# A state space mixer's step pipeline: the masked products of two token tiles side by side, y and z made one step later

## The chip, the cores and the metric

The kernel runs on one core of a Trainium2 chip, as one launch. The metric is the device time of that launch in microseconds, median of three runs. The engines' names are those of the profile: PE (matrix products; PEld its weight loads), DVE (vector), ACT (scalar), POOL (GpSimd), SP (issues the DMAs).

## The reference

Input x is 1024 tokens by 512. Four blocks follow one another, each on the layer norm of x and added to it: a linear attention read-out, a mixture of LoRA experts, a state space mixer, a second LoRA block. Nearly all of the time, and the whole change, is in the third:

```python
proj = hidden_states @ in_proj_w.T
gate, hBC, dt = proj[..., :INTER], proj[..., INTER:INTER + CONV_DIM], proj[..., INTER + CONV_DIM:]
hBC = silu(causal_conv_4_taps(hBC))          # x (8192), B and C (8 groups of 128 each)
dt = softplus(dt + dt_bias);  A_dt = -exp(A_log) * dt;  x_dt = x * dt
Y_diag = einsum('bclsh,bcshp->bclhp', (C B^T) * L, x_dt)      # masked product inside a chunk of 128
Y_off  = einsum('bclhn,bchpn->bclhp', C, states_of_earlier_chunk) * exp(A_cumsum)   # across product
y = Y_diag + Y_off + D * x
y = rmsnorm(y) * norm_w * silu(gate)
return y @ out_proj_w.T
```

## The kernel before

**Groups and steps.** The mixer has 128 heads of 64 columns in 8 groups. One group is 18 column tiles of 128 of the input projection (B, C, 8 of x, 8 of the gate) and two halves of 8 heads. The kernel runs a hand-written pipeline over the groups: a lead of 8 steps (`kind` "lead"), then 16 steps `s` for each group `g` ("first", six times "middle", "last"). A step is one token tile `t = s % 8` of one half of the heads, together with a share of the projection of tiles that the following steps and the next group need. All five engines run the same loop of steps, each with its own list of what it does in a step, and they meet only through counted semaphores. Within an engine all is done in the order written.

**PE in step s.** `turn(s + 1)`: four transposes of x into PSUM bank 6 (L1827). `diag(s)`: the masked product of this token tile, 8 heads with 64 weight columns each, in two column halves of the array, into bank 4 (L1837; the trace has 16 rows, since each of these fp32 products is two). In odd steps `across(s)`: the product with the state of the earlier chunk, four products of 128 columns into bank 5 (L1854). Then one projection tile, `project`: 24 products of 512 columns into a bank pair of 0 to 3 (L203 to L205). Last `add_up(s - 1)`: the output product of the token tile before, 8 products with z_h (L1865, L1866) and four with z_l (L1869), into bank 7. Steps 10 and 12 have a second projection tile behind it (`PROJECTED`, tiles 11 and 14). Steps 14 and 15 also hold `within` (L1916) and the across part of C B^T (L1963) for the next group.

**DVE in step s.** `add_out(s - 2)` adds bank 7 to the sum (L1569). `times_dt(s + 1)` (L1580), in steps 1 and 9 the low part of the output weights, `wo_low` (L1587), then the three taps of the convolution of a projected tile, `taps` (L1558). Then y of this token tile: in odd steps the across product is scaled (L1641), D x and the masked product are added (4 of L1653), in odd steps also the across part (L1663), and z = y times gate (L1669). Then `mask(s + 2)` (L1602). In steps 10 and 12 the taps of a second tile follow (the table `LATE`: tiles 10 and 13).

**ACT in step s.** Eviction of the projected tile (`evict`, L1300 or L1308) and the high part of the weights of tile m + 2 (`w_high`, L1288); in steps 1 and 9 `wo_high` (L1333); `decay(s + 2)` (L1321, L1326); silu of the convolved tile after DVE's taps (L1312); for `LATE` tiles eviction and w_high once more; the square of y (L1394) and z_h, the high part of z (L1397).

**POOL in step s.** The low part of the weights for each tile of `EARLY[s] + LATE[s]` (`w_low`, L1215, which waits for ACT's w_high), then z_l (L1236, which waits for z_h), three additions of squares, and in odd steps the chunk-end weights (L1225).

```python
PROJECTED = [[n] for n in range(10)] + [[10, 11], [12], [13, 14], [15], [16], [17]]
EARLY = [[-1]] + [[n] for n in range(10)] + [[11], [12], [14], [15], [16]]
LATE = [[]] * 10 + [[10], [], [13], [], [], []]
```

Of the kernel before, what the change touches and what calls it, by code (L numbers as in the profile page):

```python
# [45 lines left out]
def f(ap):  # L46

    return ap.bitcast(F32)
# [730 lines left out]
def ssm_block(nc, ctx, sems, n, x_saved, ident, bank, acc, xh, xl, xdt, w_bufs, w_in, w_dt, par, dt_bias, a_log, w_out,  # L779
# [9 lines left out]

    def sb(name, shape, dt=F32):  # L790
        return ctx.enter_context(nc.sbuf_tensor("m_" + name, shape, dt))
# [234 lines left out]

    def has_tile(kind, m):

        return kind != "last" if m >= LEAD else kind != "lead"
# [37 lines left out]
    with nc.Block() as block:  # L1067
        @block.sync
        def _(sp):
# [88 lines left out]
            def step(g, s, kind):  # L1158
# [9 lines left out]
                if own(kind) and ahead(kind, s + ROW_BUFS):  # L1168
                    sp.wait_ge(diag_done, at(g, s))
                    load_rows(g, s + ROW_BUFS)  # L1170
# [5 lines left out]
                if s % 2 == 1 and own(kind) and ahead(kind, s + 4):  # L1176
                    sp.wait_ge(y_ready, at(g, s))
                    load_e(g, s + 4)
# [12 lines left out]
        def _(pool):  # L1191
# [36 lines left out]

            def step(g, s, kind):
                t = s % NT  # L1230
# [3 lines left out]
                if own(kind):  # L1234
                    pool.wait_ge(zh_ready, at(g, s))
                    nc.gpsimd.tensor_tensor(z_l[:, s % 2, :, :], zg[:], f(z_h[:, s % 2, :, :]),  # L1236
                                            ALU.subtract).then_inc(zl_ready, 1)
                    pool.wait_ge(sq_ready, at(g, s))
                    nc.gpsimd.tensor_tensor(ysq[:, 0:2, :], ysq[:, 0:2, :], ysq[:, 2:4, :],
                                            ALU.add).then_inc(sq_pair, 1)  # L1240
                    pool.wait_ge(sq_pair, g * STEPS + (s + 1))
                    nc.gpsimd.tensor_tensor(sq_acc[:, t, :], sq_acc[:, t, :], ysq[:, 0, :],
                                            ALU.add).then_inc(sq_first, 1)
                    pool.wait_ge(sq_first, g * STEPS + (s + 1))
                    nc.gpsimd.tensor_tensor(sq_acc[:, t, :], sq_acc[:, t, :], ysq[:, 1, :],
                                            ALU.add).then_inc(sq_summed, 1)
# [37 lines left out]
        def _(act):  # L1284
# [77 lines left out]

            def step(g, s, kind):
# [27 lines left out]
                if own(kind):  # L1391
                    act.wait_ge(y_ready, at(g, s))
                    act.wait_ge(sq_summed, at(g, s - 1))
                    nc.scalar.activation(ysq[:], y[:], ACT.Square).then_inc(sq_ready, 1)  # L1394
                    act.wait_ge(z_ready, at(g, s))
                    act.wait_ge(out_done, at(g, s - 2))
                    nc.scalar.activation(z_h[:, s % 2, :, :], zg[:], ACT.Copy).then_inc(zh_ready, 1)  # L1397
# [66 lines left out]
        def _(dve):  # L1464
# [126 lines left out]
            def cb_evict(part):  # L1591
                nc.vector.tensor_tensor(cb[:, part * CT:(part + 1) * CT, :],
                                        bank[:, 5, :].rearrange("p (b c) -> p b c", c=P),
                                        causal[:].unsqueeze(1).to_broadcast([P, CT, P]),
                                        ALU.mult).then_inc(cb_ready, 1)
# [8 lines left out]

            def step(g, s, kind):
# [7 lines left out]
                if s == 0 and own(kind):  # L1613
                    nc.vector.tensor_copy(par_dn[:], par_all[:, bass.ds(g, 1), CONV_PAR:PAR].rearrange(
                        "p a b -> p (a b)")).then_inc(dn_par_ready, 1)
                    dve.wait_ge(dn_par_ready, g + 1)
# [5 lines left out]
                if s == STEPS - 1 and kind != "last":  # L1622
                    dve.wait_ge(cb_last_done, g + 2)
                    cb_evict(1)
                if ahead(kind, s + 1) and s != STEPS - 1:
                    times_dt(g, s + 1)
                if own(kind) and t == 1:
# [8 lines left out]
                if own(kind):  # L1636
                    if s % 2 == 1:
                        dve.wait_ge(off_done, pair(g, s))
                        dve.wait_ge(e_loaded[s // 2 % 2], (g * 4 + (s // 4 + 1)) * 32)
                        off = e[:, s // 2 % 2, :, :]  # L1640
                        nc.vector.tensor_tensor(off, bank[:, 5, :].rearrange("p (c l) -> p c l", c=CT), off,  # L1641
                                                ALU.mult).then_inc(off_ready, 1)
                    dve.wait_ge(diag_done, at(g, s))
                    dve.wait_ge(ecs_stored, 16)
                    dve.wait_ge(sq_ready, at(g, s - 1))
                    dve.wait_ge(z_ready, at(g, s - 1))
                    whole = bank[:, 4, :].rearrange("p (c l) -> p c l", c=CT)
                    by_tensor = kind == "last" and half == 1
                    if by_tensor and s % 2 == 0:
                        last = nc.vector.tensor_copy(y[:], whole)  # L1650
                    for ct in range(0 if by_tensor else CT):
                        d = half * CT + ct
                        last = nc.vector.scalar_tensor_tensor(  # L1653
                            out=y[:, ct, :], in0=xc[:, half, ct, t * P:(t + 1) * P], scalar=par_dn[:, d:d + 1],
                            in1=bank[:, 4, ct * P:(ct + 1) * P], op0=ALU.mult, op1=ALU.add)
                    if by_tensor and s % 2 == 1:
                        dve.wait_ge(off_ready, pair(g, s))
                        last = nc.vector.tensor_tensor(y[:], whole, off, ALU.add)
                    elif s % 2 == 1:
                        last.then_inc(dx_added, 1)  # L1660
                        dve.wait_ge(dx_added, g * (STEPS // 2) + (s // 2 + 1))
                        dve.wait_ge(off_ready, pair(g, s))
                        last = nc.vector.tensor_tensor(y[:], y[:], off, ALU.add)  # L1663
                    last.then_inc(y_ready, 1)
                    dve.wait_ge(y_ready, at(g, s))
                    dve.wait_ge(zl_ready, at(g, s - 1))
                    if t == 0:
                        dve.wait_ge(gate_done, gate_at(g, half * LEAD - 1))
                    nc.vector.tensor_tensor(zg[:], y[:], gate[:, half, :, t * P:(t + 1) * P],  # L1669
                                            ALU.mult).then_inc(z_ready, 1)  # L1670
# [135 lines left out]
        def _(pe):  # L1806
# [24 lines left out]
            def diag(g, s):  # L1831
                pe.wait_ge(mt_ready, at(g, s))
                pe.wait_ge(xdt_ready, at(g, s))
                pe.wait_ge(y_ready, at(g, s - 1))
                for h in range(UH):
                    row = (h % 2) * SP_
                    last = nc.tensor.matmul(bank[row:row + SP_, 4, (h // 2) * P:(h // 2 + 1) * P],  # L1837
# [279 lines left out]
```

## Time and profile before

| | |
|---|---|
| median of 3 runs | 1736.9 us (1736.45 to 1739.39) |
| the profiled execution, its own time | 1737.69 us |
| its span, first to last instruction | 1735.9 us |
| mean granted TensorE clock | 0.987 |
| busy: PE, PEld, DVE, ACT, POOL | 1684.0, 1378.6, 1190.5, 1269.4, 732.2 us |
| PE's share of the chain that ended last | 81% |

A row of a timeline gives the start in us from the span's beginning, the length, the engine, the line in the kernel, what is written and read, and how many instructions were merged; in brackets the idle time of the engine before it and who ended it. "L1837 128*64" is a product that uses half of the array's columns. Rows of the clock view give the granted share of TensorE's clock in a stretch: 1.00 is 2.4 GHz, 0.50 is 1.2 GHz.

### The profile page before, as it was taken

What the parts mean: (1) busy time and instruction counts of PE and PEld (TensorE: products, weight loads), DVE (VectorE), ACT (ScalarE), POOL (GpSimd) and SP (SyncE); (2) the same over time, 40 slices, a digit from 0 to 9 for tenths busy, and PEclk for the clock granted to TensorE, in tenths of its full rate; (3) what the DMA queues carried; (4) which work ended last, traced back from release to release, by engine and by line L of the source; (5) the groups of instructions that cost most, each with busy time, mean ns of one, the idle gap of its engine ahead of it and who ended that gap; (6) DMA issues with size and microseconds to landing.
All of it is one profiled execution on the core that took longest, in us unless ns stands there. A gap on an engine that the chain in (4) does not pass through costs nothing.

```text
span 1735.9 us, 26827 instructions
## 1 busy us (share of the span) xinstructions
PE 1684.0 (97%) x9484; PEld 1378.6 (79%) x9484; DVE 1190.5 (69%) x1846; ACT 1269.4 (73%) x2171; POOL 732.2 (42%) x792
## 2 busy tenths in 40 slices
PE   6998799999999999999999999999999999999999
PEld 5876577888888888888888888888888888888877
DVE  5665676767676767667776767676767676767785
ACT  4333148987888779877987798778887889688851
POOL 3553122544344334443444444434443444344470
PEclk9998799999999999999999999999999999999999
DMA  4320225423232323332333232323232233223311
GB/s 170 109 68 1 75 65 159 122 93 105 86 112 85 117 74 111 95 109 83 113 93 107 78 110 88 116 88 109 94 110 78 86 115 104 90 79 115 105 70 49
DMA packets 98564, 166.46 MB, mean 96 GB/s; under 512 B 11616, under 2 KB 49888, under 8 KB 96768
## 3 DMA queue, kind: packets, MB, share of 16 engines
q1 hardware_dynamic: 98432, 164.75, 29.7%
q8 instruction: 76, 1.25, 0.3%
q14 instruction: 56, 0.46, 0.1%
HBM read 158.43 MB, written 6.29 MB: 95 GB/s over the span
## 4 chain that ended last, share of the span: by engine, by line
PE 81%; DVE 4%; ACT 2%; issue 1%; DVEq 0%; ACTq 0%
PE bank L203 15%; PE bank L205 15%; PE bank L204 15%; PE bank L1837 7%; PE bank L1865 7%; PE bank L1866 7%; PE bank L1869 7%; PE bank L1854 4%; PE bank L1827 3%; PE bank L1916 1%; DVE m_xc L1558 1%; DVE m_gate L1558 0%; PE bank L1845 0%; ACT m_mt L1321 0%; DVE m_xc L1492 0%
## 5 line engine op out<-in xcount | busy, mean ns | idle before, releaser
L203 PE MATMUL bank<-xh,w_h 128*128 128x512 f32 x1152 | 463.3, 402 | 3.4 <-DVE m_xc L1558 2.9
L205 PE MATMUL bank<-xh,w_l 128*128 128x512 f32 x1152 | 451.8, 392 | 0.0
L204 PE MATMUL bank<-xl,w_h 128*128 128x512 f32 x1152 | 449.4, 390 | 0.0
L1236 POOL TENSOR_TENSOR m_z_l<-m_zg,m_z_h 128x512 fp32r<-128x512 f32 x128 | 177.6, 1387 | 568.6 <-ACT m_z_h L1397 568.6
L1321 ACT ACTIVATE m_mt<-m_mt,m_unit 128x128 f32<-128x128 f32 x1024 | 312.1, 390 | 0.0
L1215 POOL TENSOR_TENSOR w_l<-w_raw,w_h 128x512 fp32r<-128x512 f32 x144 | 187.7, 1303 | 230.9 <-ACT w_h L1288 230.9
L1569 DVE TENSOR_TENSOR x<-x,bank 128x512 f32<-128x512 f32 x128 | 87.8, 686 | 264.5 <-PE bank L1869 264.5
L203 PEld LDWEIGHTS bank<-xh,w_h 128*128 128x128 f32 x1152 | 216.8, 188 | 55.7 <-issue 13.6
L205 PEld LDWEIGHTS bank<-xh,w_l 128*128 128x128 f32 x1152 | 216.5, 188 | 47.3
L1558 DVE SCALAR_TENSOR_TENSOR m_xc<-bank,m_par_conv,m_xc 128x1020 f32<-128x1020 f32 (+2 forms) x192 | 244.6, 1274 | 10.4 <-ACT m_xc L1300 5.4
L204 PEld LDWEIGHTS bank<-xl,w_h 128*128 128x128 f32 x1152 | 217.1, 188 | 41.7
L1865 PE MATMUL bank<-m_wo_h,m_z_h 128*128 128x512 f32 x512 | 203.8, 398 | 1.3 <-DVE x L1569 1.3
L1866 PE MATMUL bank<-m_wo_l,m_z_h 128*128 128x512 f32 x512 | 202.5, 396 | 0.0
L1602 DVE TENSOR_TENSOR m_mt<-m_mt,m_cb 128x1024 f32<-128x1024 f32 x128 | 156.9, 1225 | 26.1 <-ACT m_mt L1326 26.0
L1837 PE MATMUL bank<-m_mt,xdt 128*64 128x128 f32 x2048 | 140.1, 279 | 0.1
L1869 PE MATMUL bank<-m_wo_h,m_z_l 128*128 128x512 f32 x512 | 138.5, 392 | 0.0
L1326 ACT ACTIVATE m_mt<-m_mt 128x1024 f32<-128x1024 f32 x128 | 135.8, 1061 | 2.2
L1653 DVE SCALAR_TENSOR_TENSOR m_y<-m_xc,m_par_dn,bank 128x128 f32<-128x128 f32 x480 | 133.9, 342 | 1.5 <-PE bank L1837 1.5
L1837 PEld LDWEIGHTS bank<-m_mt,xdt 128*64 128x64 f32 x2048 | 109.2, 136 | 21.5 <-issue 20.5
L1580 DVE TENSOR_TENSOR xdt<-bank,m_unit 128x512 f32<-128x512 f32 x128 | 87.8, 686 | 49.5 <-issue 48.6
L1326 ACT ACT_TABLE_LOAD x93 | 119.3, 1283 | 1.6
L1865 PEld LDWEIGHTS bank<-m_wo_h,m_z_h 128*128 128x128 f32 x512 | 96.1, 188 | 24.2 <-ACT m_z_h L1397 1.3
(275 smaller groups left out, 2781.0 us busy)
## 6 DMA issues: line engine op xcount, KB each, us to landing
m_mt<-ncs_rows SPq DMA_DIRECT2D x128, 512.0 KB, 3.7
w_raw<-w_in SPq DMA_DIRECT2D x144, 256.0 KB, 3.0
m_wo_raw<-w_out_in SPq DMA_DIRECT2D x64, 256.0 KB, 5.1
m_e<-ecs_rows SPq DMA_DIRECT2D x128, 128.0 KB, 3.5
a_wo_raw<-wo_in SPq DMA_DIRECT2D x8, 1024.0 KB, 4.9
x<-x_in SPq DMA_DIRECT2D x8, 256.0 KB, 4.6
a_wq_raw<-wq_in SPq DMA_DIRECT2D x8, 256.0 KB, 4.1
x_saved<-x SPq DMA_DIRECT2D x1, 2048.0 KB, 9.1
```

Source lines behind the costliest of these rows:

```text
L203: nc.tensor.matmul(out, ah, bh, start=first, stop=False)
L204: nc.tensor.matmul(out, ah, bl, start=False, stop=False)
L205: return nc.tensor.matmul(out, al, bh, start=False, stop=last)
L1215: nc.gpsimd.tensor_tensor(w_l[:, m % 2, :, :], w_raw[:, m % W_BUFS, :, :], f(w_h[:, m % 2, :, :]), ALU.subtract).then_inc(w_split, 1)
L1236: nc.gpsimd.tensor_tensor(z_l[:, s % 2, :, :], zg[:], f(z_h[:, s % 2, :, :]), ALU.subtract).then_inc(zl_ready, 1)
L1321: last = nc.scalar.activation(mt[:, s % ROW_BUFS, h, :], mt[:, s % ROW_BUFS, h, :], ACT.Relu, bias=own_row)
L1326: nc.scalar.activation(slot, slot, ACT.Exp, scale=-1.0).then_inc(decay_ready, 1)
L1558: ins = nc.vector.scalar_tensor_tensor(out=dst[:, :, back:], in0=src[:, :, 0:length - back], scalar=par_conv[:, w:w + 1], in1=dst[:, :, ba ...
L1837: last = nc.tensor.matmul(bank[row:row + SP_, 4, (h // 2) * P:(h // 2 + 1) * P], xdt[:, s % 2, h * SP_:(h + 1) * SP_], mt[:, s % ROW_BUFS, ...
L1865: nc.tensor.matmul(bank[:, 7, :], z_h[:, s % 2, ct, :], wo_h[:, ct, :], start=ct == 0, stop=False)
L1866: nc.tensor.matmul(bank[:, 7, :], z_h[:, s % 2, ct, :], wo_l[:, ct, :], start=False, stop=False)
L1869: last = nc.tensor.matmul(bank[:, 7, :], z_l[:, s % 2, ct, :], wo_h[:, ct, :], start=False, stop=ct == CT - 1)
```

## The change

It holds for every group but the second half of the last one (`paired` is true). The arithmetic is the same.

1. PE: no masked product in an even step; the odd step does those of s - 1 and s, in banks 4 and 5 (`masked_in`).
2. The across product goes to bank 7, the output product's; it waits until bank 7 was added (`acc_added`), and the next output product waits until the across product was scaled (`off_ready`).
3. y and z of tile s - 1 are made in step s on DVE, ahead of times_dt and the taps; square and z_h on ACT in step s behind the decay and ahead of silu; z_l and the squares' sums on POOL in step s, behind `w_low` of `EARLY[s] + LATE[s]` (`made_in`). `add_up(s - 1)` stays in step s.
4. `within`, both parts, and the across part of C B^T stand in the middle of the projection of step 14.
5. In the last group's second half the old order stands; its step 8 makes y and z of tiles 7 and 8.

```diff
+    def paired(kind, s):
+        return not (kind == "last" and s >= NT)
+    def masked_in(kind, s):
...
+        if paired(kind, s):
+            return [s - 1, s] if s % 2 == 1 else []
+        return [s]
+    def made_in(kind, s):
...
+        if paired(kind, s):
+            return [s - 1] if behind(kind, s - 1) else []
+        return [s - 1, s] if s == NT else [s]
+    def across_bank(kind, s):
+        return 7 if paired(kind, s) else 5
...
@@ POOL
             def step(g, s, kind):
-                t = s % NT
                 for m in EARLY[s] + LATE[s]:
                     if has_tile(kind, m) and has_tile(kind, m + 2):
                         w_low(g, m + 2)
-                if own(kind):
-                    pool.wait_ge(zh_ready, at(g, s))
...
+                for made in made_in(kind, s):
+                    split_and_square(g, made)
@@ ACT
+                if paired(kind, s):
+                    for made in made_in(kind, s):
+                        square_and_high(g, made)
                 for m in EARLY[s]:
                     if has_tile(kind, m) and is_conv[m % TILES]:
                         silu(g, m)
...
                     if has_tile(kind, m):
                         evict(g, m)
                         w_high(g, m + 2)
-                if own(kind):
-                    act.wait_ge(y_ready, at(g, s))
...
+                if not paired(kind, s):
+                    for made in made_in(kind, s):
+                        square_and_high(g, made)
@@ DVE
-                if s == STEPS - 1 and kind != "last":
-                    dve.wait_ge(cb_last_done, g + 2)
-                    cb_evict(1)
+                if paired(kind, s):
+                    for made in made_in(kind, s):
+                        make_y(g, made)
+                        make_z(g, made)
+                    if own(kind) and s % 2 == 1:
+                        scale_across(g, s, kind)
                 if ahead(kind, s + 1) and s != STEPS - 1:
                     times_dt(g, s + 1)
...
@@ PE
             def diag(g, s):
...
-                pe.wait_ge(y_ready, at(g, s - 1))
+                by_tensor = g == LAST and s >= NT
+                to_bank = 4 if by_tensor else 4 + s % 2
+                if s == STEPS - 2 and not by_tensor:
+                    pe.wait_ge(cb_ready, g * 2 + 4)
+                pe.wait_ge(y_ready, at(g, s - 1 if by_tensor and s > NT else s - 2))
...
+            def across(g, s, kind):
...
+                if paired(kind, s):
+                    pe.wait_ge(acc_added, at(g, s - 2))
...
             def add_up(g, s):
...
+                if s % 2 == 0 and not (g == LAST and s >= NT):
+                    pe.wait_ge(off_ready, pair(g, s + 1))
...
             def step(g, s, kind):
...
-                if own(kind):
-                    diag(g, s)
...
+                for ready in masked_in(kind, s):
+                    diag(g, ready)
+                if own(kind) and s % 2 == 1:
+                    across(g, s, kind)
```

PE, a middle group: how an odd step begins. L1827 and L1888 are the transposes, L1837 and L1902 the masked products, L1854 and L1922 the across products. Before:

```order
L205 MATMUL bank<-xh,w_l 128x512
L1827 MATMUL bank<-ident,m_xc 128x128 x4
L1837 MATMUL bank<-m_mt,xdt 64x128 x8
L1854 MATMUL bank<-m_cb_across,m_xdd 128x128 x4
L203 MATMUL bank<-xh,w_h 128x512
```

Now:

```order
L204 MATMUL bank<-xl,w_h 128x512
L205 MATMUL bank<-xh,w_l 128x512
L1888 MATMUL bank<-ident,m_xc 128x128 x4
L1902 MATMUL bank<-m_mt,xdt 64x128 x16
L1922 MATMUL bank<-m_cb_across,m_xdd 128x128 x4
```

The masked products of two token tiles stand in a row; the even step has none (there the transposes are followed by the projection).

ACT, step 10 from its decay to the eviction of the next step (m_mt the decay, m_ysq the square of y, m_z_h the high part of z, the evictions read bank, silu reads and writes m_gate). Before:

```order
L1321 ACTIVATE m_mt<-m_mt,m_unit 128x128 x8
L1326 ACTIVATE m_mt<-m_mt 128x1024
L1312 ACT_TABLE_LOAD
L1312 ACTIVATE m_gate<-m_gate 128x1024
L1300 ACTIVATE m_gate<-bank,m_par_conv 128x1024
L1288 ACTIVATE w_h<-w_raw 128x512
L1394 ACTIVATE m_ysq<-m_y 128x512
L1397 ACTIVATE m_z_h<-m_zg 128x512
L1312 ACTIVATE m_gate<-m_gate 128x1024
L1308 ACTIVATE m_gate<-bank 128x1024
```

Now:

```order
L1352 ACTIVATE m_mt<-m_mt,m_unit 128x128 x8
L1357 ACTIVATE m_mt<-m_mt 128x1024
L1397 ACTIVATE m_ysq<-m_y 128x512
L1400 ACTIVATE m_z_h<-m_zg 128x512
L1343 ACT_TABLE_LOAD
L1343 ACTIVATE m_gate<-m_gate 128x1024
L1331 ACTIVATE m_gate<-bank,m_par_conv 128x1024
L1319 ACTIVATE w_h<-w_raw 128x512
L1343 ACTIVATE m_gate<-m_gate 128x1024
L1339 ACTIVATE m_gate<-bank 128x1024
```

Square and z_h have moved ahead of silu; they are now those of tile 9, and before those of tile 10. The second eviction and w_h (for projection tile 12) stand behind both.

POOL, the end of step 9 and step 10, now (L1245 is w_low, L1263 z_l):

```order
L1255 TENSOR_TENSOR m_xdd<-xdt,m_unit 128x512
L1245 TENSOR_TENSOR w_l<-w_raw,w_h 128x512 x2
L1263 TENSOR_TENSOR m_z_l<-m_zg,m_z_h 128x512
L1266 TENSOR_TENSOR m_ysq<-m_ysq 128x256
L1268 TENSOR_TENSOR m_sq_acc<-m_sq_acc,m_ysq 128x128
```

The rows of POOL read the same before, with other line numbers; what moved is which tile they belong to. The z_l behind the two w_l (of projection tiles 11 and 12) is that of tile 9, which PE's step 10 uses; before it was that of tile 10, which PE's step 11 uses.

## Rows read from the trace of the kernel before

**Rows 1.** The page: busy time of each engine.
```profile
PE 1684.0 (97%) x9484; PEld 1378.6 (79%) x9484; DVE 1190.5 (69%) x1846; ACT 1269.4 (73%) x2171; POOL 732.2 (42%) x792
```

**Rows 2.** Waits of PE: us in total, times, longest.
```profile
PE bank L1916 <- DVE m_cb L1592: 1.0, 1, 1.0
```

**Rows 3.** Timeline of PE, an odd step (start, length); then step 1 of a half.
```profile
902.61 0.60 PE L1827 MATMUL bank<-ident,m_xc 128*128 128x128 f32 x4
903.14 1.09 PE L1837 MATMUL bank<-m_mt,xdt 128*64 128x128 f32 x16
904.16 1.16 PE L1854 MATMUL bank<-m_cb_across,m_xdd 128*128 128x128 f32 x8
...
923.35 0.60 PE L1827 MATMUL bank<-ident,m_xc 128*128 128x128 f32 x4
...
931.38 0.40 PE L1865 MATMUL bank<-m_wo_h,m_z_h 128*128 128x512 f32 x1
```

**Rows 4.** Lines L1837 and L1854, idle of PEld before them: us, times.
```profile
  issue: 20.5, 120
...
  issue: 9.1, 53
```

**Rows 5.** Timeline of PE, step 10: transposes, first product with z_h, with z_l.
```profile
934.16 0.60 PE L1827 MATMUL bank<-ident,m_xc 128*128 128x128 f32 x4
...
941.30 0.40 PE L1865 MATMUL bank<-m_wo_h,m_z_h 128*128 128x512 f32 x1
...
943.17 1.08 PE L1869 MATMUL bank<-m_wo_h,m_z_l 128*128 128x512 f32 x4
```

**Rows 6.** Timeline of DVE: y and z of an odd tile; the taps in step 10.
```profile
928.00 1.12 DVE L1653 SCALAR_TENSOR_TENSOR m_y<-m_xc,m_par_dn,bank 128x128 f32<-128x128 f32 x4
...
929.88 0.69 DVE L1669 TENSOR_TENSOR m_zg<-m_y,m_gate 128x512 f32<-128x512 f32 x1
...
935.57 3.89 DVE L1558 SCALAR_TENSOR_TENSOR m_gate<-bank,m_par_conv,m_gate 128x1020 f32<-128x1020 f32 x3
```

**Rows 7.** Timeline of ACT: z_h in step 1; silu, late eviction, w_high in step 10.
```profile
931.30 0.62 ACT L1397 ACTIVATE m_z_h<-m_zg 128x512 fp32r<-128x512 f32 x1
...
939.50 1.06 ACT L1312 ACTIVATE m_gate<-m_gate 128x1024 f32<-128x1024 f32 x1 [1.23 <-DVE m_gate L1558]
941.50 1.21 ACT L1300 ACTIVATE m_gate<-bank,m_par_conv 128x1024 f32<-128x1024 f32 x1 [0.94 <-PE bank L205]
942.62 0.61 ACT L1288 ACTIVATE w_h<-w_raw 128x512 fp32r<-128x512 f32 x1
```

**Rows 8.** Timeline of POOL, step 10.
```profile
943.31 1.30 POOL L1215 TENSOR_TENSOR w_l<-w_raw,w_h 128x512 fp32r<-128x512 f32 x1 [5.97 <-ACT w_h L1288]
944.56 1.29 POOL L1236 TENSOR_TENSOR m_z_l<-m_zg,m_z_h 128x512 fp32r<-128x512 f32 x1
```

**Rows 9.** Timelines of ACT and PE, first group: square of step 0, first output product, decay of step 1.
```profile
302.08 0.61 ACT L1394 ACTIVATE m_ysq<-m_y 128x512 f32<-128x512 f32 x1
...
309.13 0.40 PE L1865 MATMUL bank<-m_wo_h,m_z_h 128*128 128x512 f32 x1
...
312.18 1.06 ACT L1326 ACTIVATE m_mt<-m_mt 128x1024 f32<-128x1024 f32 x1
```

**Rows 10.** Timeline of PE: the last long wait within a projection.
```profile
262.57 0.47 PE L203 MATMUL bank<-xh,w_h 128*128 128x512 f32 x1 [2.90 <-DVE m_xc L1558]
```

**Rows 11.** Stretches: length, busy of PE, PEld, DVE, ACT, POOL, granted clock, DMA, GB/s.
```profile
181.19:188.01 6.82, 6.45 (x19) 4.51 (x18) 4.43 (x8) 1.20 (x2) 0.00 (x0) 0.50 0.00 0
263.11:266.52 3.41, 3.41 (x10) 2.64 (x9) 3.34 (x9) 2.02 (x3) 1.28 (x1) 0.50 0.10 33
```

**Rows 12.** Timelines of DVE, ACT and PE, last group, step 8 (it begins at 1632.20).
```profile
1632.20 0.60 PE L1827 MATMUL bank<-ident,m_xc 128*128 128x128 f32 x4
...
1633.00 0.69 DVE L1580 TENSOR_TENSOR xdt<-bank,m_unit 128x512 f32<-128x512 f32 x1
...
1634.66 0.48 PE L1865 MATMUL bank<-m_wo_h,m_z_h 128*128 128x512 f32 x1
```

More of the change, by code:

```diff
@@ L1635, in step @@
                     cb_evict(0)
-                if own(kind):
[L1637 to L1670, printed above, removed]
@@ L1671, in step @@
+                    dve.wait_ge(cb_last_done, g + 2)
+                    cb_evict(1)
+                if not paired(kind, s):
+                    for made in made_in(kind, s):
+                        if made % 2 == 1 and made == s:
+                            scale_across(g, made, kind)
+                        make_y(g, made)
+                        make_z(g, made)
                 if kind == "lead" and s == STEPS - 1:
@@ L1847, in diag @@
                 last.then_inc(diag_done, 1)
-            def across(g, s):
+            def across(g, s, kind):
                 pe.wait_ge(cb_across_ready, g + 1)
@@ L1922, in step @@
                     turn(g, s + 1)
-                if own(kind):
-                    diag(g, s)
-                if s == STEPS - 2 and kind != "last":
-                    pe.wait_ge(silu_done, conv_at(g, C_TILE))
-                    pe.wait_ge(off_ready, pair(g, s - 1))
-                    within(0).then_inc(cb_first_done, 1)
-                if own(kind) and s % 2 == 1 and s != STEPS - 1:
-                    across(g, s)
-                todo = [m for m in PROJECTED[s] if has_tile(kind, m)]
@@ new lines, in step @@
+                if own(kind) and s % 2 == 1:
+                    across(g, s, kind)
+                todo = [m for m in PROJECTED[s] if has_tile(kind, m)]
+                for m in todo[:1]:
+                    project(g, m, 0)
+                    if s == STEPS - 2 and kind != "last":
+                        pe.wait_ge(silu_done, conv_at(g, C_TILE))
+                        if own(kind):
+                            pe.wait_ge(y_ready, at(g, s - 1))
+                        else:
+                            pe.wait_ge(packed_ready, 3)
+                        within(0).then_inc(cb_first_done, 1)
+                        within(1).then_inc(cb_last_done, 1)
+                        pe.wait_ge(xdt_ready, at(g, s + 1))
+                        for b in range(SEQS):
+                            first = b * CHUNKS * P
+                            last = nc.tensor.matmul(bank[:, 6, b * P:(b + 1) * P], b_cm[:, first:first + P],
+                                                    c_cm[:, first + P:first + 2 * P], start=True, stop=True)
+                        last.then_inc(cb_across_done, 1)
+                    project(g, m, 1)
@@ L1949, in step @@
+                if s == STEPS - 1 and kind != "last":
+                    pe.wait_ge(cb_across_ready, g + 2)
+                    turn(g, s + 1)
                 if behind(kind, s - 1):
```

152 lines of the change are left out of this document (91 added, 61 removed).

## The prediction

> **What bounds the kernel now.** First the page's busy line: PE is busy for 1684.0 us of a span of 1735.9, the next engine, ACT, for 1269.4 [rows 1]. Then PE's list of waits: what is left in the mixer is next to nothing, the largest single one there being 1.0 us in the lead, before the second `within` [rows 2]. So in the mixer's steps PE never waits, and two things alone can move the time: what PE itself does, and new waits of PE. For the first I read PE's timeline step by step [rows 3], for the second the timelines of DVE, ACT and POOL in the steps where PE's next operand comes last [rows 5 to 8].
>
> **What the pairing saves.** The masked products use half of the array's columns (128*64), their neighbours all of them. Where the shape changes, the weight load, otherwise hidden under the running product, has to wait: 20.5 us over 120 entries, 0.17 us each [rows 4]. The way out costs the same: 9.1 us over the 53 across products that come right behind, again 0.17 each [rows 4]. So of the 1.02 us from the first masked product to the first across product [rows 3] the batch itself takes 0.85. Now two batches share one entry and one exit: 0.34 us for each pair of steps. Pairs: seven groups of 8 and the first half of the last, 60. **-20.4 us.** The number of products stays. By the other side: nothing (0), if the cost were not in the change of shape; at most the 0.53 from transposes to masked products plus 0.17, 42 us. I take 20.4, since the row counts just this wait.
>
> Here a rule of the skill speaks otherwise. The Trainium skill, page "TensorE: Matmul & The Clock Gate", section "Architectural detail: the array is 16× 32×32, not 1× 128×128", says that PE can pull a weight load ahead of matrix products in flight. By that alone a change of shape would cost no time and this term would be 0; rows 4 speak against it between these two shapes, and the case is a rival below.
>
> **Moved at no price.** `within` and the across part of C B^T go into the middle of step 14's projection; products of 128 columns between products of 512 cost their own time only, before as after. The 1.0 us wait in the lead goes, as both parts now have a bank of their own: **-1.0**. The across product's new wait for bank 7: add_out takes 0.69 us from the step's start, the across product starts some 2.4 us into the step (0.53 + 0.85 + 1.02 [rows 3]): covered by 1.4 us. The output product's wait for `off_ready` is covered by the whole projection. SP loads the rows of two tiles together in the odd step, still a step ahead of the decay that reads them.
>
> **The new waits: y and z a step behind.** Before, z_h and z_l of tile s - 1 were made in step s - 1 and used in step s. Now they are made in the very step whose output product uses them. When is that? An even step now has no masked products: its output product starts 1.2 us earlier than today's 7.14 us after the transposes (941.30 - 934.16 [rows 5]; 1.2 is 1.02 and the 0.17 of the entry), at 5.93; its z_l part 1.87 later (943.17 - 941.30), at **7.80 us**. An odd step's starts at 8.03 + 0.85 = 8.88 [rows 3].
>
> z_h is in time: in step 1, where ACT has wo_high ahead, z_h ends at 931.92, 8.57 us after that step's start [rows 3, 7], 0.31 before 8.88. In the other steps I find 0.2 us and more.
>
> z_l is not, in steps 10 and 12. POOL's list for the step is first the low weights of `EARLY` and `LATE`, then z_l, and POOL takes them in order: at 943.31 it waits 5.97 us for ACT's w_high, then come w_l and z_l [rows 8]. Today that z_l is for the next step of PE; now it is for this one. The chain that ends it, from the step's start:
> - DVE's taps ended at 939.46, 5.30 after the start [rows 5, 6]. Ahead of them now stand y and z of the odd tile: 1.88 for y (929.88 - 928.00) and 0.60 for z before the next may start, 2.48. Taps end at 7.78.
> - ACT: silu 1.06, which has stayed ahead of the late eviction, then eviction 1.21 (1.12 to the next start), w_high 0.61 [rows 7]: 10.6.
> - POOL: w_l 1.25 to the start of z_l, 1.29 for z_l [rows 8]: 13.2.
>
> PE needs it at 7.80 and stands for **5.4 us**. Behind it on PE stand the rest of the output product, the second projection tile and the whole next step; nobody else can fill in. Bounds: if ACT's eviction came right after the projection (no silu ahead), z_l would end at 5.9 + 0.2 + 1.21 + 0.61 + 1.30 + 1.29 = 10.5, a wait of 2.7; with another table load of ACT (about 1.3) on the chain, 6.7. I take 5.4. This happens in steps 10 and 12 of the groups that have late tiles, the first seven: 14 x 5.4 = **+75.6**.
>
> **The clock behind a wait.** After PE waited 2.90 us for DVE [rows 10], the granted clock was 0.50 (1.2 GHz) for 3.41 us of unbroken projection; behind a wait of 3.8 us in the experts' block it was 0.50 for 6.82 us [rows 11]. Half of such a stretch is lost: 1.7 or 3.4 us. I take 1.7, since the work behind is the same kind, for each of the 14 waits: **+23.8**. Bounds: 0 (no fall) and 3.4 each.
>
> **Start and end.** In the first group, step 1, ACT is late already: the decay's end, 313.24, less the square and z_h that leave step 0 (1.15, from 302.08 on), is 312.1; then square and z_h to 313.1. PE would come to its first output product at 309.13 - 1.0 - 1.2 + 0.85 = 307.8 [rows 9]. A wait of 5.3, and 1.7 of clock: **+7.0**. In the last group's step 8, where no projection covers, y of tile 7 starts after times_dt, 1.4 us into the step, z ends at 3.9, z_h at 4.7; the output product stood at 2.46 [rows 12]: **+2.2**.
>
> **The sum**: -20.4 - 1.0 + 75.6 + 23.8 + 7.0 + 2.2 = +87.2 on the profiled execution's 1737.7, 1824.9. That execution lies 0.8 above the median, so against the median the forecast is **1824 us**.
>
> **Rivals.**
> - *z_l isn't held (faster).* Place: POOL's queue in steps 10 and 12. If z_l, whose own operand is ready at about 4 us, went past the w_l that waits, PE would get it at 5.3 and stand nowhere there. Then -20.4 - 1.0 + 7.0 + 2.2 = -12.2: 1725. It decides below a wait of 12.2 / 14 = 0.87 us a step. For it: the semaphore z_l waits for is set early. Against it: the row of POOL at 944.56 starts only when w_l is through, although z_h had ended at 944.27, and the order of POOL's instructions is as written. Chance 0.04.
> - *The clock doesn't fall*: 15 x 1.7 less, 1799. For it: PE has long been at full clock before each wait. Against: the fall behind a wait of only 2.90 [rows 10, 11]. 0.15.
> - *The clock falls for the longer stretch*: 3.4 each, 1850. The waits here are longer than the 3.8 us that was followed by 6.82. 0.10.
> - *Further waits for z_h* in steps 1, 4, 6 and 9, where I find 0.2 to 0.4 us of slack: half a microsecond in each, 32 times, +16: 1840. 0.10.
> - *The shape costs nothing*: the 0.17 us before those weight loads would be something else that stays, and 20.4 are missing from the sum: 1844. Against it: rows 4 show the wait at each of 120 entries and nowhere between products of one shape. 0.03. (This is what the Trainium skill's rule above would make of it.)
> - The forecast itself: 0.56. Left over for what I don't see: 0.02.
>
> **How the numbers follow.** The range takes in the two cases of the clock, the further waits and the free change of shape, with 2 us for the other terms: 1797 to 1852. Only the first rival is outside it, as is some of the uncertainty of the 5.4. A measurement can tell 0.2%, 3.5 us. Faster by more: the first rival, 0.04. Within: 0.01. Slower: 0.95.
>
> **What would show it.** Right: in PE's list of waits a new line of some 70 us, 14 times or so, at the z_l part of the output product, released by POOL's z_l; ahead of it POOL waiting for ACT's w_high in steps 10 and 12; idle before L1837's weight loads halved to about 60 times 0.17; granted clock 0.50 in short stretches twice a group. Wrong: no such line, or one of under a microsecond each; a wait at the z_h part in many steps; idle before the masked products as large as before.

## The result, and the profile after

The changed kernel takes **1841.3 us** (median of 4 runs, 1840.17 to 1842.51), the one before, run beside it, 1737.15 us (4 runs, 1736.45 to 1739.39). The ratio is 1.0596, with a 95% interval of 1.058 to 1.0613: slower by 104 us. The forecast was 1824, with a range of 1797 to 1852.

The page of the changed kernel: busy time of each engine, and the chain that ended last.

```profile
PE 1706.1 (93%) x9484; PEld 1402.7 (76%) x9484; DVE 1196.1 (65%) x1846; ACT 1266.9 (69%) x2171; POOL 753.4 (41%) x792
...
PE 72%; DVE 9%; ACT 3%; issue 3%; POOL 2%; DVEq 0%; ACTq 0%
```

The counts of instructions are those of [rows 1] to the last one. No work was added; the span grew by 102.5 us to 1838.4 while PE's busy time grew by 22. Most of what came is time in which PE stands, and some is the same work at a lower clock.

Span and mean granted clock:

```profile
core 0: 1838.4 us, clock 0.961
```

It was 0.987 before. Now the waits of PE, then of its weight loads (PEld): us in total, times, longest. L1940 is the product with z_l, L1936 the first with z_h, L1902 the masked products, L1922 the across product, L1888 the transposes.

```profile
PE bank L1940 <- POOL m_z_l L1263: 73.3, 14, 5.4
...
PE bank L1936 <- ACT m_z_h L1400: 6.8, 2, 4.8
...
PE bank L203 <- DVE m_xc L1596: 3.7, 2, 2.9
...
PEld bank L1902 <- issue: 11.8, 61, 0.4
...
PEld bank L1922 <- issue: 10.3, 60, 0.2
...
PEld bank L1888 <- ACT m_xc L1343: 3.8, 8, 0.5
```

One line is new and large: 14 waits, 73.3 us, for z_l. The second has two members, one of 4.78 in the first group and one of 1.97 in the last. Below them the weight loads before the masked products and before the across product wait 61 and 60 times; before, there were 120 entries [rows 4] and as many exits: 53 into the across product [rows 4], 60 into a projection, 7 into `within`. The last line is small and new too: once a group the transposes wait for a late silu.

The wait itself, in step 10 of a middle group (the step begins at 977.00). PE (start, length, engine, instruction, and in brackets the idle time before and who ended it):

```profile
977.00 0.60 PE L1888 MATMUL bank<-ident,m_xc 128*128 128x128 f32 x4
...
982.93 0.40 PE L1936 MATMUL bank<-m_wo_h,m_z_h 128*128 128x512 f32 x1
...
990.32 2.07 PE L1940 MATMUL bank<-m_wo_h,m_z_l 128*128 128x512 f32 x4 [5.35 <-POOL m_z_l L1263]
992.19 0.63 PE L203 MATMUL bank<-xh,w_h 128*128 128x512 f32 x1
```

DVE, the same step: y, z, then the taps of the late projection tile:

```profile
977.80 1.12 DVE L1665 SCALAR_TENSOR_TENSOR m_y<-m_xc,m_par_dn,bank 128x128 f32<-128x128 f32 x4
...
979.89 0.69 DVE L1685 TENSOR_TENSOR m_zg<-m_y,m_gate 128x512 f32<-128x512 f32 x1
...
981.10 3.89 DVE L1596 SCALAR_TENSOR_TENSOR m_gate<-bank,m_par_conv,m_gate 128x1020 f32<-128x1020 f32 x3
```

ACT: z_h, silu behind the taps, the late eviction, w_high:

```profile
980.62 0.63 ACT L1400 ACTIVATE m_z_h<-m_zg 128x512 fp32r<-128x512 f32 x1
...
985.02 1.06 ACT L1343 ACTIVATE m_gate<-m_gate 128x1024 f32<-128x1024 f32 x1 [2.48 <-DVE m_gate L1596]
985.99 1.19 ACT L1331 ACTIVATE m_gate<-bank,m_par_conv 128x1024 f32<-128x1024 f32 x1
987.08 0.62 ACT L1319 ACTIVATE w_h<-w_raw 128x512 fp32r<-128x512 f32 x1
```

POOL: w_l, and only then z_l:

```profile
987.77 1.27 POOL L1245 TENSOR_TENSOR w_l<-w_raw,w_h 128x512 fp32r<-128x512 f32 x1 [8.46 <-ACT w_h L1319]
989.00 1.26 POOL L1263 TENSOR_TENSOR m_z_l<-m_zg,m_z_h 128x512 fp32r<-128x512 f32 x1
```

z and z_h are through at 981.25. z_l needs nothing else, but starts 7.75 us later, behind a w_l that waits 8.46 us for a chain of taps, silu, eviction and w_high. PE wanted z_l 7.97 us into the step (990.32 - 5.35 - 977.00) and got it at 13.3.

Last, the clock. Three stretches (length, busy PE, PEld, DVE, ACT, POOL, granted clock, DMA share, GB/s), the first from just before the end of the wait above:

```profile
989.48:996.31 6.83, 5.99 (x14) 4.73 (x15) 2.28 (x3) 1.06 (x1) 2.38 (x4) 0.50 0.29 78
1184.04:1187.45 3.41, 3.33 (x8) 2.66 (x9) 1.56 (x2) 1.06 (x1) 1.62 (x4) 0.50 0.56 148
310.23:317.05 6.82, 4.35 (x10) 3.47 (x11) 1.23 (x1) 6.78 (x15) 4.17 (x6) 0.50 0.11 40
```

Behind 10 of the 14 waits for z_l the granted clock is 0.50 (1.2 GHz) for 6.83 us, behind the other 4 for 3.41; the third stretch is that of the first group's wait.

### The profile page after: what moved, and what is told of

Its sections match the earlier page's. It is cut to its first block, busy times and chain, and to the rows that moved or that the text cites. A ratio compares the mean times of both kernels' runs of the same rounds, so it can differ in the third digit from the quotient of the medians.

```text
span 1838.4 us, 26891 instructions
## 1 busy us (share of the span) xinstructions
PE 1706.1 (93%) x9484; PEld 1402.7 (76%) x9484; DVE 1196.1 (65%) x1846; ACT 1266.9 (69%) x2171; POOL 753.4 (41%) x792
## 3 DMA queue, kind: packets, MB, share of 16 engines
q8 instruction: 76, 1.25, 0.3%
## 4 chain that ended last, share of the span: by engine, by line
PE 72%; DVE 9%; ACT 3%; issue 3%; POOL 2%; DVEq 0%; ACTq 0%
PE bank L203 13%; PE bank L205 13%; PE bank L204 13%; PE bank L1940 7%; PE bank L1902 6%; PE bank L1936 6%; PE bank L1937 6%; PE bank L1922 4%; PE bank L1888 3%; DVE m_xc L1596 2%; DVE m_gate L1596 2%; POOL w_l L1245 1%; POOL m_z_l L1263 1%; DVE m_y L1665 1%; PE bank L1985 1%
## 5 line engine op out<-in xcount | busy, mean ns | idle before, releaser
L203 PE MATMUL bank<-xh,w_h 128*128 128x512 f32 x1152 | 471.2, 409 | 4.2 <-DVE m_xc L1596 3.7
L205 PE MATMUL bank<-xh,w_l 128*128 128x512 f32 x1152 | 459.0, 398 | 0.0
L204 PE MATMUL bank<-xl,w_h 128*128 128x512 f32 x1152 | 456.1, 396 | 0.0
L1263 POOL TENSOR_TENSOR m_z_l<-m_zg,m_z_h 128x512 fp32r<-128x512 f32 x128 | 174.9, 1366 | 484.5 <-ACT m_z_h L1400 484.5
L1245 POOL TENSOR_TENSOR w_l<-w_raw,w_h 128x512 fp32r<-128x512 f32 x144 | 186.8, 1297 | 385.4 <-ACT w_h L1319 385.4
L203 PEld LDWEIGHTS bank<-xh,w_h 128*128 128x128 f32 x1152 | 223.3, 194 | 48.5 <-issue 5.5
L204 PEld LDWEIGHTS bank<-xl,w_h 128*128 128x128 f32 x1152 | 223.3, 194 | 44.3
L1940 PE MATMUL bank<-m_wo_h,m_z_l 128*128 128x512 f32 x512 | 153.5, 425 | 73.3 <-POOL m_z_l L1263 73.3
L1936 PE MATMUL bank<-m_wo_h,m_z_h 128*128 128x512 f32 x512 | 205.7, 402 | 8.5 <-ACT m_z_h L1400 6.8
L1940 PEld LDWEIGHTS bank<-m_wo_h,m_z_l 128*128 128x128 f32 x512 | 102.7, 204 | 102.7 <-POOL m_z_l L1263 79.4
L1343 ACT ACTIVATE m_xc<-m_xc 128x1024 f32<-128x1024 f32 x64 | 67.9, 1061 | 115.6 <-DVE m_xc L1596 115.5
L1331 ACT ACTIVATE m_xc<-bank,m_par_conv 128x1024 f32<-128x1024 f32 x64 | 76.6, 1196 | 73.6 <-PE bank L205 73.6
L1902 PE MATMUL bank<-m_mt,xdt 128*64 128x128 f32 x2048 | 126.8, 276 | 0.0
L1936 PEld LDWEIGHTS bank<-m_wo_h,m_z_h 128*128 128x128 f32 x512 | 96.8, 189 | 33.1 <-ACT m_z_h L1400 8.6
```

Of the source, the lines that this page charges most:

```text
L203: nc.tensor.matmul(out, ah, bh, start=first, stop=False)
L204: nc.tensor.matmul(out, ah, bl, start=False, stop=False)
L205: return nc.tensor.matmul(out, al, bh, start=False, stop=last)
L1245: nc.gpsimd.tensor_tensor(w_l[:, m % 2, :, :], w_raw[:, m % W_BUFS, :, :], f(w_h[:, m % 2, :, :]), ALU.subtract).then_inc(w_split, 1)
L1902: last = nc.tensor.matmul(bank[row:row + SP_, to_bank, (h // 2) * P:(h // 2 + 1) * P], xdt[:, s % 2, h * SP_:(h + 1) * SP_], mt[:, s % ROW ...
L1936: nc.tensor.matmul(bank[:, 7, :], z_h[:, s % 2, ct, :], wo_h[:, ct, :], start=ct == 0, stop=False)
```

## The experiments

The theory: POOL's order holds z_l back in steps 10 and 12, the wait is as long as the chain of ACT ahead of w_l, and the clock falls because PE stands. The rivals: the wait has another cause (DVE's taps, or y and z themselves being late); the lost clock comes from something else than the standing; and what was gained is not the change of shape but something else in the pairing.

### POOL's order alone

```diff
-                for m in EARLY[s] + LATE[s]:
+                for m in EARLY[s]:
                     if has_tile(kind, m) and has_tile(kind, m + 2):
                         w_low(g, m + 2)
                 for made in made_in(kind, s):
                     split_and_square(g, made)
+                for m in LATE[s]:
+                    if has_tile(kind, m) and has_tile(kind, m + 2):
+                        w_low(g, m + 2)
```

> The changed kernel with one edit: in POOL's steps 10 and 12 the low weights of the late tile stand behind z_l instead of ahead of it. Theory (z_l is held in POOL's queue by the w_low that waits for ACT): all 14 waits for z_l, 73 us, go, and with them the half clock behind them; left are the saving of the pairing (-20.4), the two waits for z_h (4.8 and 2.0) and some 5 us of clock behind these: 1728 to 1730 us, below the kernel before. Rival 1 (z itself is late, POOL's order does not matter): 1841 stays. Rival 2 (the next in line takes the place: the second projection tile waits for DVE's taps, or the late w_low comes too late for tile 12): the z_l line goes, another of 1 us or more in each of the 14 steps comes, 1745 to 1780.

Measured: **1735.83 us** (1734.78 to 1737.86) against 1739.16 for the kernel before beside it; ratio 0.9986 (0.9977 to 0.9995). The largest waits of its mixer, and the span:

```profile
PE bank L1939 <- ACT m_z_h L1403: 6.7, 2, 4.8
...
PE bank L1988 <- DVE m_y L1678: 1.2, 7, 0.2
```

```profile
core 0: 1734.3 us, clock 0.982
```

The whole line of 73.3 us is gone, and with it 104.1 us of the span, 30.8 more than the line itself. So the order of two entries in one engine's list made the change's whole loss, and with it put right the rest of the change stands 0.14% below the kernel before (0.05 to 0.23), some 2 us.

The length of a step (from its first transpose to the next step's) says more than the spans. Steps 10 and 12 of the seven groups last 307.4 us together in the changed kernel and 199.1 here: 108.3 less, of which 73.3 are the waits and 35.0, 2.5 for each wait, came on top of them. Of these 2.5, 0.17 still belong to the wait: its row counts from the modelled end of the product before (0.40 long), while in a stream the next one starts 0.23 after it. The other 2.3 are left for the clock.

The gain is smaller than expected (1728 to 1730 us). The two z_h waits came as expected, 11.8 us with their low clock: step 1 of the first group lasts 18.73 us where it takes 11.69 in other groups, steps 8 and 9 of the last group 16.49 where they took 11.61 before, 7.0 and 4.9 more. These two take back over half of the gain from pairing. The miss is in three things that nobody had counted. One is new in this kernel:

```profile
PEld bank L1988 <- issue: 3.9, 7, 0.6
```

L1988 is `within` in step 14. It waits for y of tile 13, which DVE now makes in that same step. From the first transpose of step 14 to the transposes of step 15 it is 20.32 us here and 19.92 in the changed kernel, where PE had stood in step 12 and DVE was further ahead. That is 0.4 in each of seven groups, 2.9 in all. The other two, a late silu (2.1) and one more stretch of low clock behind the last group (1.7), stand in the changed kernel too and are told below.

### PE kept busy through the wait

22 more output products go between the z_h and the z_l part in steps 9 and 11 of `add_up` (the output tiles of steps 10 and 12), into a bank that nobody reads. Nothing else changes, and the z_l chain stays as it is.

```diff
+                if s in (9, 11) and g < LAST:
+                    pe.wait_ge(y_ready, at(g, s - 1))
+                    for i in range(22):
+                        nc.tensor.matmul(bank[:, 4, :], z_h[:, s % 2, i % CT, :], wo_h[:, i % CT, :], start=True, stop=True)
                 pe.wait_ge(zl_ready, at(g, s))
```

> The changed kernel, with 22 further products of 512 columns on PE in steps 10 and 12 of the first seven groups, between the z_h and the z_l part, into a bank that nobody reads then. They end about when z_l comes (22 x 0.23 = 5.0 us, the waits are 5.13 to 5.35). They add no length to the step if PE waited anyway. Theory (the fall of the clock behind the wait costs some 2.7 us each time): the granted clock stays at 1.00 through the groups, 1841 less 14 x 2.7 = 38, so about 1803. Rival (the clock costs nothing beyond what the waits cost, the other 43 us are something else, the saving of the pairing missing for instance): 1841. The forecast's own 1.7 each would give 1817.

Measured: **1810.6 us** (1809.41 to 1811.15), ratio 1.041 (1.0396 to 1.0424). Span and clock, and the longer half of what is left of the wait (the other 7 are 0.08 us each):

```profile
core 0: 1808.5 us, clock 0.983
```

```profile
PE bank L1944 <- POOL m_z_l L1263: 1.9, 7, 0.3
```

14 x 22 products at 0.233 us are 71.8 us, with 2.5 of waits left 74.3: as much time passes in these places as before (73.3). Yet the kernel is 30.7 us quicker than the changed one (1841.3 - 1810.6), and none of the 14 places has a stretch of low clock behind it. The mixer's low stretches that are left stand behind the two z_h waits, of the first group (at 310.95) and of the last (at 1703.59), which this edit doesn't touch. PE does 308 products more and ends sooner. So the second part of the loss is the clock, and it is the standing that brings it: 30.7 + 1.0 = **31.7 us, 2.3 for each wait**. That is less than the 2.7 of the expectation and more than the forecast's 1.7. The steps of the first experiment give the same 2.3. Its span gives 30.8 in all, but that is no second measurement: 2.9 us of a new wait had come in there.

### Two changes of shape again

The first experiment's kernel, with the across product put between the two batches of masked products: the same instructions, and one exit and one entry more for each pair.

```diff
-                for ready in masked_in(kind, s):
+                for ready in masked_in(kind, s)[:1]:
                     diag(g, ready)
                 if own(kind) and s % 2 == 1:
                     across(g, s, kind)
+                for ready in masked_in(kind, s)[1:]:
+                    diag(g, ready)
```

> The previous kernel (late low weights behind z_l) with the across product between the two batches of masked products in the odd step, so that PE changes between half and all columns as often as in the kernel before. Everything else stands as it was. Theory (0.17 us on each entry and each exit, 60 pairs): 20.4 us more than that kernel. Rival (a change of shape costs nothing, weight loads are pulled ahead): the same time within 2 us.

Measured: **1754.48 us** (1752.7 to 1755.38), ratio 1.0087 (1.0073 to 1.01): 18.65 us over the first experiment's kernel, 0.31 for each of 60 pairs, where 0.34 was forecast. The steps show the price itself. Where steps 5 and 6 of a middle group begin, in the first experiment and then here:

```profile
881.01 0.60 PE L1891 MATMUL bank<-ident,m_xc 128*128 128x128 f32 x4
892.70 0.60 PE L1891 MATMUL bank<-ident,m_xc 128*128 128x128 f32 x4
```

```profile
889.47 0.60 PE L1891 MATMUL bank<-ident,m_xc 128*128 128x128 f32 x4
901.50 0.60 PE L1891 MATMUL bank<-ident,m_xc 128*128 128x128 f32 x4
```

The odd step takes 12.03 us in place of 11.69: **0.34 us** for one more exit and entry, and the even steps are alike. It is so in seven of a middle group's eight pairs. In the eighth nothing is added, since this kernel no longer has the 0.4 us wait of `within` in step 14 (its loads wait 0.2 there in place of 0.6); nor in the first group's first pair, where the z_h wait is shorter by as much. With 52 pairs at 0.34 the sum would be 17.7. That the time gives 18.65 is in part chance: the last group's steps 8 and 9 take 1.2 us more, the work ahead of the mixer's first group 0.8 more, that behind the last group 1.35 less. The waits of this kernel's weight loads:

```profile
PEld bank L203 <- issue: 16.5, 61, 3.3
...
PEld bank L1905 <- issue: 12.8, 67, 0.4
...
PEld bank L1925 <- issue: 10.3, 60, 0.2
```

The first line was 6.9 us in 8 waits in the first experiment; the projection's first load now waits where the second batch ends, as it should. The second grew only from 11.8 in 61 to 12.8 in 67: the entry behind the across product idles 0.12 us, too little for this list, so the lengths of the steps are the better witness. They settle that what pairing saves is the change between 128*64 and 128*128. The Trainium skill, page "TensorEngine Tiling (Array Packing)", section "Key Properties", says that a change of tiling mode drains TensorE; it gives no price. The 0.34 us of each odd step agree with it. The rule weighed in the prediction, of loads pulled ahead, doesn't hold across that change.

### Silu behind the late eviction

The changed kernel, with ACT's late eviction and w_high ahead of silu. POOL's order stays.

```diff
-                for m in EARLY[s]:
-                    if has_tile(kind, m) and is_conv[m % TILES]:
-                        silu(g, m)
                 for m in LATE[s]:
                     if has_tile(kind, m):
                         evict(g, m)
                         w_high(g, m + 2)
+                for m in EARLY[s]:
+                    if has_tile(kind, m) and is_conv[m % TILES]:
+                        silu(g, m)
```

> The changed kernel with ACT's silu of the early tile behind the late tile's eviction and w_high in steps 10 and 12. Theory (the chain that ends z_l is taps, silu, eviction, w_high, w_low, z_l): the taps and silu drop out of it, eviction comes right behind the projection, each wait shrinks from 5.2 to about 2.7 us, 35 us less, and 0 to 2.7 us of clock each less: 1770 to 1806. Rival (silu is not on the chain, for instance because DVE's z or POOL itself is late): 1841 stays.

Measured: **1806.32 us** (1803.67 to 1808.97), ratio 1.0386 (1.0372 to 1.04). The wait, then POOL and DVE in one such step:

```profile
PE bank L1940 <- POOL m_z_l L1263: 48.4, 14, 3.6
```

```profile
595.09 1.21 DVE L1640 TENSOR_TENSOR m_mt<-m_mt,m_cb 128x1024 f32<-128x1024 f32 x1
...
595.12 2.32 POOL L1245 TENSOR_TENSOR w_l<-w_raw,w_h 128x512 fp32r<-128x512 f32 x1 [5.63 <-ACT w_h L1319]
```

The chain through taps and silu is confirmed: without it w_high ends about 2.8 us sooner against PE's need. But 3.5 us of wait are left where 2.7 were expected. The reason stands in the rows: w_l takes 2.32 us in place of 1.27, and starts together with DVE's mask. So it is in all 14 steps: 2.30 to 2.32 us in step 10, where the two run together for 1.2 us, and 2.10 in step 12, where for 1.0. That puts the time at the upper end of what was expected, 0.3 beyond it. Of the 35.0 us gained, 24.9 are the wait and 10 the clock. Behind 13 of the 14 waits the low stretch is now 3.41 us; behind the first group's first wait, as long as the others (3.55), there is none. What follows that wait, and what follows the next group's first (length, busy time of the engines, granted clock, DMA share, GB/s):

```profile
412.72:417.72 5.00, 5.00 (x22) 4.11 (x23) 1.96 (x3) 1.06 (x1) 1.56 (x3) 1.00 0.33 101
598.75:602.16 3.41, 3.41 (x8) 2.73 (x9) 2.02 (x3) 1.06 (x1) 1.51 (x3) 0.50 0.48 142
```

The step with the one lasts 18.04 us, with the other 19.63.

### The mask behind the taps

The same, and in steps 10 and 12 DVE's mask moved behind the late taps, away from w_l.

```diff
-                if ahead(kind, s + 2):
+                if ahead(kind, s + 2) and not LATE[s]:
                     mask(g, s + 2)
...
                     if has_tile(kind, m):
                         taps(g, m)
+                if ahead(kind, s + 2) and LATE[s]:
+                    mask(g, s + 2)
```

> The kernel with silu behind the late eviction, with DVE's mask (an operation of 1.2 us on the on-chip memory alone) moved behind the late tile's taps in steps 10 and 12, so that it no longer runs beside POOL's late w_low. Theory (w_low took 2.3 us instead of 1.3 in these steps because the mask ran beside it): w_low is back at 1.3 us, the wait for z_l falls from 3.45 to 2.4 us in each of the 14 steps, 15 us less wait and a little clock, 1785 to 1792. Rival (w_low is slow there for another reason): the wait stays at 3.45, 1806.

Measured: **1783.95 us** (1782.19 to 1788.72), ratio 1.026 (1.0241 to 1.0279). The wait, w_l, and the stretch behind the first and the second wait of one group:

```profile
PE bank L1942 <- POOL m_z_l L1263: 35.3, 14, 2.5
```

```profile
591.98 1.27 POOL L1245 TENSOR_TENSOR w_l<-w_raw,w_h 128x512 fp32r<-128x512 f32 x1 [5.64 <-ACT w_h L1319]
```

```profile
594.00:599.00 5.00, 4.46 (x19) 3.68 (x20) 3.52 (x4) 1.33 (x2) 3.11 (x4) 1.00 0.40 108
624.50:627.90 3.40, 3.40 (x9) 2.63 (x8) 1.61 (x2) 0.94 (x1) 1.32 (x1) 0.50 0.22 60
```

w_l takes 1.27 us again and the wait is 2.5, near the 2.4 expected. The low clock now follows one wait of each group and not the other, though both last 2.52 us. This gives the price of one such stretch directly: step 10, without it, lasts 17.0 us, step 12, with it, 18.6, and in the first experiment, where neither waits, both last 14.22. So a stretch of 3.41 us costs 1.6. Steps 10 and 12 of all groups together are 21.5 us shorter than with the mask in its old place, 13.1 of that by the waits. The time is just below the 1785 to 1792 expected.

### Both ends mended

The first experiment's kernel, with the two z_h waits that it leaves taken up: in the first group's step 1 ACT makes the square and z_h of tile 0 ahead of wo_high and the decay; in the last group tile 7's y and z are made in step 7, where the projection covers them (on DVE behind `scale_across`, so that the across product isn't held up).

```diff
         if paired(kind, s):
-            return [s - 1] if behind(kind, s - 1) else []
-        return [s - 1, s] if s == NT else [s]
+            made = [s - 1] if behind(kind, s - 1) else []
+            return made + [s] if kind == "last" and s == NT - 1 else made
+        return [s]
...
+                if kind == "first" and s == 1:
+                    square_and_high(g, 0)
                 if own(kind) and t == 1:
...
-                if paired(kind, s):
+                if paired(kind, s) and not (kind == "first" and s == 1):
                     for made in made_in(kind, s):
                         square_and_high(g, made)
```

> The kernel with the late low weights behind z_l, and two more edits: in the first group's step 1 ACT squares y and makes z_h of tile 0 ahead of wo_high and the decay; in the last group tile 7's y and z are made in step 7, not in step 8. Theory (the 4.8 us wait in the first group is ACT's queue, the 2.0 us in the last is y made too late, and each has half clock behind it): the first shrinks to below 1 us, the second goes, and 1 to 3.4 us of clock behind each: 8 to 11 us less than that kernel's 1735.8, so 1725 to 1728. Rival (other waits, for the low part of the output weights in the first group and for DVE in the last, stand right behind them): less than 3 us are won.

Measured: **1729.76 us** (1729.31 to 1730.27, 6 runs) against 1739.81; ratio 0.9945 (0.9931 to 0.9958). Waits, and the last group's output product:

```profile
PE bank L1944 <- DVE m_wo_l L1631: 2.2, 2, 1.9
...
PE bank L1944 <- ACT m_z_h L1404: 0.6, 1, 0.6
```

```profile
1629.47 0.47 PE L1944 MATMUL bank<-m_wo_h,m_z_h 128*128 128x512 f32 x1 [1.88 <-DVE m_wo_l L1631]
```

The first group's wait falls from 4.76 to two pieces, 0.6 for wo_low in step 1 and 0.65 for z_h in step 2, and its low stretch is gone: that group is 4.4 us shorter than in the first experiment. In the last group the wait only changes its name: 1.88 for wo_low, which DVE makes late there, in place of 1.97 for z_h. Its low stretch stays, and steps 8 and 9 together win only 0.65. So 5 us are won, where 8 to 11 were expected, and the rival of the expectation holds for the last group. (The span is 6.7 us shorter; the rest of that lies in work ahead of the mixer's groups and behind them, which is the same in both.) Still this is the fastest version, 0.55% below the kernel before.

## Why the prediction was right, and where its terms were off

The case came out as forecast: the wait is in its place, with its cause, and the sign and the range hold. By its steps:

- **The z_l waits**: forecast 14 x 5.4 = 75.6, measured 73.3 in 14 waits of 5.35 and 5.13 by turns. The chain, from the step's start: taps end at 7.99 (forecast 7.78), z_l at 13.26 (13.2), needed at 7.97 (7.80). The rival that z_l isn't held falls by POOL's rows.
- **The clock** is the term that was mis-sized: "I take 1.7 ... for each of the 14 waits", 23.8 in all. Measured 31.7, 2.3 each. I took the shorter of two observed stretches, since the work behind was the same kind; in fact 10 of the 14 were of the longer. Where the shorter followed (4 waits) 1.6 us were lost, as forecast. A stretch of 6.83 us doesn't cost half its length, since it begins while PE still stands (989.48, the wait ends at 990.32): behind 6 waits it took 2.9 us, behind 4, where it began 2.2 us before the wait's end, 2.2.
- **The start**: forecast 5.3 of waiting and 1.7 of clock, 7.0; measured 4.78 of waiting, and by the length of step 1 (18.70 against 11.69 in other groups) 7.0 in all. **The end**: forecast 2.2, measured 4.9 (steps 8 and 9 together last 16.51, before 11.61). The wait of 1.97 is as forecast; I had no term for the 3.41 us of low clock behind it (1.7), nor for step 9, where loads of the output product wait for wo_low and 1.1 us more are lost.
- **Pairing**: forecast -20.4 from 0.34 a pair. Steps 2 and 3 together take 20.41 us, before 20.74, and the third experiment puts 0.34 back: the term holds. The rival that the shape costs nothing falls by the same experiment.
- **The lead's wait** of 1.0 [rows 2] is gone as forecast, but 0.8 us of waiting for the taps stands in its place (in the line L203 for m_xc above); the lead is 0.4 us shorter, not 1.0.
- **Moved at no price** holds for the changed kernel. In the first experiment's kernel `within`, in its new place, waits 0.4 us in each of seven groups for y, made one step later: two parts of the change that meet only once the waits for z_l are gone.
- **Further z_h waits** in steps 1, 4, 6 and 9, other than the first group's: none. The 0.2 to 0.4 us of slack held.
- **Not seen**: the moved square and z_h put one of ACT's silus (of a tile of x) later in one step of each group, and the transposes' loads wait 0.48 us for it, 3.8 us of load time over 8 groups (the PEld line above). On PE about 0.2 us of each remains in step 6 (the transposes start 1.13 us behind the start of the z_l part there, and 0.92 elsewhere) and 0.06 in step 7: 2.1 in all.
- **Not seen, and its cause open**: from the last group's step 14 to the end the same work takes 70.01 us, before 68.11. The mixer's last steps, its output and the second LoRA block lie there. A stretch of the same kind of products, some 24 us behind the last long wait of PE, before and then after the change:

```profile
1711.30:1714.71 3.41, 3.41 (x32) 3.41 (x31) 1.96 (x4) 1.40 (x3) 0.00 (x0) 1.00 0.11 41
1812.09:1815.50 3.41, 3.41 (x18) 3.41 (x17) 1.29 (x2) 0.80 (x2) 0.00 (x0) 0.50 0.01 4
```

PE is busy throughout in both, and no row shows a wait of it over 0.15 us between. The kernel before and the third and the last experiment lack this low stretch; all the others have it. Why it comes is open.

By place, then, the span's 102.5 us add up. Steps 10 and 12 are 108.3 longer than without the waits, the first group's start 7.0, the last group's steps 8 and 9 4.9, the late silu 2.1, behind the last group 1.9, the pairing -20.4, and all ahead of the first group -1.0 (0.6 of it in blocks that the change doesn't touch): 102.8. Against the forecast's 87.2 these are 15.6 more: 8.9 in steps 10 and 12 (2.3 less in the waits' own rows, 11.2 more on top of them), 2.7 at the end, 2.1 for the silu and 1.9 behind the last group.

## What to carry to other kernels

When the work of a step is made later by one step, walk every engine's list for entries that waited harmlessly ahead of it: here a w_l that used to wait 6 us at no cost stood in front of the one result that had lost its slack, and the fix was two entries in another order. Price a wait on TensorE with what the clock does behind it: here 2.3 us on top of each 5.2. And cost a gain and its delays apart: the pairing saves 20 us and was hidden under a loss of 104. With that loss put right it could be kept, though the smaller new waits leave the kernel only 0.14% below the one before, and 0.55% once the first group's is mended too.

## What the runs showed of the hardware

- The low clock isn't in proportion to the wait. After 5.13 to 5.35 us of standing it was 6.83 us long behind 10 waits and 3.41 behind 4; after 3.35 to 3.57 us it was 3.41 behind 13 waits, with none behind one; after 2.52 us it was 3.41 behind 7 and none behind the other 7. With PE kept fed for the same time (second experiment) there was none. So making a wait shorter can be worth more than what it is shortened by: the mask's move took 13.1 us from the waits and 21.5 from the steps in which they stand.
- One stretch of 3.41 us at 1.2 GHz cost 1.6 us: 18.6 against 17.0 for steps that both wait 2.52 us, and 19.63 against 18.04 for steps that both wait 3.55.
- POOL's w_l (128x512, from SBUF to SBUF) took 2.32 us beside DVE's mask (128x1024, SBUF only) and 1.27 us when the mask was moved away; the mask took 1.21 to 1.25 us either way. Where the two ran together for 1.2 us w_l lost 1.05, where for 1.0 it lost 0.83. That the two meet is shown by the move; over which resource, no run here tells.
- The change between 128*64 and 128*128 costs PE 0.34 us for the way in and out (12.03 against 11.69 us for the odd step). The way from the across product into the projection, both 128*128, has no such wait in the rows.
